# Inverse roots on GpSimd, rows copied earlier, merged weights computed in four parts of the layer before

## Chip, cores, metric

One core of one Trainium2 chip. The metric is the device time of one execution of the whole program in microseconds (us), the median of several runs; lower is better.

## What is computed

x is (8, 512, 128) in float32. First a small recurrent layer, then six layers of windowed attention and a gated feed-forward block. Cut to what matters:

```python
h = tanh(h @ A.T + xb_t); y = h @ C.T                # 512 steps in sequence, with layer norms around
for i in range(6):
    t = shift_tokens(x)                              # features 64..127 from one token earlier
    q, k, v = split(t @ Wqkv[i])                     # 16 heads of 64
    q, k = l2norm(q), l2norm(k)                      # one inverse root for each token and head
    q, k = rotary(q), rotary(k)
    attn = softmax(8 * q k^T, masked to a window of 32 and the one before)
    x = (attn @ v) @ Wo[i] + x
    t = shift_tokens(x)
    n = (t - mean) / sqrt(var + 1e-5)                # one inverse root for each token
    a, g = split(n @ W1[i] + b1[i]); x = (a * gelu(g)) @ W2[i] + b2[i] + x
```

## The kernel before

Everything is held in SBUF, the engines' programs are written out by hand, and semaphores are the only order between them. Engines are called PE (TensorE), DVE (VectorE), ACT (ScalarE), POOL (GpSimd) and SP (the queue that issues DMAs).

**Recurrence.** The first 356 us are 512 steps of a small matmul on PE (L532) and a tanh on ACT (L750), in eight chunks of 64 tokens. Two filler matmuls (`keep_warm`, L517) stand in each step, or one filler and one piece of a neighbouring chunk's work (`outputs`, `turn_input`, `turn_xn`, `start_chunk`). DVE does the layer norms of the chunks beside it.

**Layers.** The work is cut into 192 tiles of 128 tokens (a window of 32 tokens of four sequences), 32 tiles a layer. A loop over steps s runs them as a pipeline: in step s tile A = s is projected and rotated, B = s-1 is normalised, turned and compared, C = s-2 goes through the softmax, E = s-3 gets its output. Four tiles make a round T, 48 in all, and after a round its feed-forward block is run in the steps that `turn_of(s, lag)` names: lag 7 the rows and their statistics, 8 the normalised rows, 9 the turn back, 10 the gate, 11 and 12 the values, 13 the second product. So four kinds of step alternate, told apart here by s mod 4: **kind 3** (rows, statistics, value part 0), **kind 0** (normalised rows, value parts 1 and 2), **kind 1** (turn back, second product), **kind 2** (gates).

Order on each engine within a step, as far as it matters:
- PE: project q of A (L552); transpose of C (L646); output of E with merged weights (L654); turn q of B (L559); project k of A (L552); turn k of B (L559); feed-forward pieces; comparisons of B (L701); softmax times inputs of C (L714).
- ACT: copies of `px` (L822), inputs, `ex` (L828), square of q (L769), copies of turned q and k (L855, L862), values (L808), square of k, feed-forward pieces (among them `xr`, L776, the rows' copy out of PSUM, kind 3), last `guess_roots` (L812, L814), the first guess of the inverse roots of tile A.
- DVE: rotate q (L954, L957), softmax sums, sum of squares of q (L963), output added (L1024), rotate k, `pT` (L1033), statistics of rows (L985, L989, kind 3, read from PSUM), update of x (L995, kind 1), sum of squares of k, maximum, `px`, `sh` (L1054), last `inverse_roots` (L970 to L978), five operations on 32 (kind 3: 36) elements in a partition that refine the guess to `rr`.
- POOL: in kind 0 `shift` (L442); B's q and k times `rr` (L448, twice); `pn` of C (L453); sum of the two rotated halves of A's q and k (L458, twice); the tables' scales (L431, kinds 1 and 3); in kind 3 variance and mean of the rows (L467, L469); `hh`, value times gate (L477: one in kind 3, two in kind 0).

**Merged weights.** `w_vo` = Wv Wo of a head is computed on PE once a layer (L664, 16 products, 32 instructions) into four PSUM banks that the turns use too, in the single step s = 32 L + 2 (`layer_of`), and copied out by ACT (L850, four copies). PE waits for the output before (`y_added`) ahead of it and for the copies behind it. `w_vo` has one buffer.

## Time and profile before

| | us |
|---|---|
| median of 3 runs (3452.42 to 3457.12) | 3455.07 |
| profiled execution, its own time | 3451.7 |
| its span, first to last instruction | 3449.9 |
| recurrence (first L552 at 358.1) | 358 |
| 192 steps of the layers, to the last L552 | 2995 |
| end of the pipeline | 97 |

Busy shares of the span: PE 96%, PE's weight loads 62%, DVE 81%, ACT 67%, POOL 65%; mean granted TensorE clock 0.989. How to read it: the page's first part gives busy time by engine; a matmul's end is modelled and its tail overlaps the next, so busy time of PE does not by itself say that PE is the bound. What says more is the order in time of a few steps, where an engine's start stands right behind what released it. Times of the trace count from the start of the span.

### The profile page before, as it was taken

Reading aid. Unit: us, or ns where it says so; the run is one execution under the profiler, and the core shown is the slowest. Engines: PE = TensorE matmul, PEld = TensorE weight load, DVE = VectorE, ACT = ScalarE, POOL = GpSimd, SP = SyncE. Lnnn points to the kernel's source line nnn. Section 1 sums busy time; section 2 is a strip of 40 time slices with the busy share of each in tenths; the row PEclk is TensorE's granted clock in tenths of the full one; section 3 lists DMA queues with packets and bytes.
Section 4 is the critical chain, followed back from the end, with each engine's and each line's share of the span. In section 5 each row is a group of like instructions: output and inputs, shape, how many; then the busy total and the mean of one; then the engine's idle time right before and its main releaser. Section 6 shows DMA issues by size and latency. Waiting matters only on the chain. (4 is left out here: it accounts for less than half of the span.)

```text
span 3449.9 us, 100942 instructions
## 1 busy us (share of the span) xinstructions
PE 3313.6 (96%) x42197; PEld 2155.7 (62%) x42197; DVE 2796.1 (81%) x4511; ACT 2308.7 (67%) x4545; POOL 2259.3 (65%) x1364
## 2 busy tenths in 40 slices
PE   8999689999999999999999999999999999999996
PEld 5555366666666666666666666666666666666663
DVE  2333698988898899898889889988888898988892
ACT  2222367777777777777777777777777777777774
POOL 0000476777777777777777677776777776777772
PEclk9999899999999999999999999999999999999998
DMA  2000000100001000001000001000001000000000
GB/s 72 1 1 1 7 11 9 36 11 11 8 17 35 11 8 11 11 17 33 11 11 11 8 17 35 11 9 10 11 17 32 11 11 11 12 13 17 14 8 13
DMA packets 62281, 52.50 MB, mean 15 GB/s; under 512 B 11526, under 2 KB 59396, under 8 KB 61828
## 3 DMA queue, kind: packets, MB, share of 16 engines
q1 hardware_dynamic: 61828, 46.05, 5.1%
q8 instruction: 335, 5.49, 0.7%
q14 instruction: 118, 0.97, 0.1%
HBM read 43.93 MB, written 2.10 MB: 13 GB/s over the span
## 5 line engine op out<-in xcount | busy, mean ns | idle before, releaser
L448 POOL TENSOR_TENSOR cosp<-cosp,rr 128x1024 f32<-128x1024 f32 x384 | 723.2, 1905 | 587.0 <-DVE rr L978 586.9
L458 POOL TENSOR_TENSOR cosp<-cosp,sinp 128x1024 f32<-128x1024 f32 x384 | 903.4, 2375 | 53.9 <-DVE sinp L957 53.7
L552 PE MATMUL ps<-w_qk,xs 128*128 128x512 f32 x1536 | 762.5, 619 | 21.0 <-ACT sq L769 17.2
L654 PEld LDWEIGHTS ps<-px,w_vo 128*128 128x128 f32 x6144 | 701.0, 192 | 57.5 <-ACT px L822 44.2
L654 PE MATMUL ps<-px,w_vo 128*128 128x128 f32 x6144 | 721.6, 276 | 2.0 <-ACT px L822 1.7
L769 ACT ACTIVATE sq<-ps 128x1024 f32<-128x1024 f32 x384 | 393.0, 1023 | 473.5 <-DVE sinp L957 473.5
L954 DVE TENSOR_TENSOR cosp<-ps,tab 128x1024 f32<-128x1024 f32 x384 | 469.2, 1222 | 143.0 <-PE ps L552 141.6
L552 PEld LDWEIGHTS ps<-w_qk,xs 128*128 128x128 f32 x1536 | 262.9, 191 | 385.9 <-issue 376.0
L963 DVE TENSOR_REDUCE ss<-sq 128x16 f32<-128x1024 f32 x384 | 455.2, 1185 | 55.0 <-ACT sq L769 54.9
L957 DVE TENSOR_TENSOR sinp<-ps,tab 128x1024 f32<-128x1024 f32 x384 | 465.9, 1213 | 0.0
L714 PE MATMUL ps<-pT,xtm 32*128 32x512 f32 x3072 | 447.6, 625 | 12.7 <-issue 5.5
L559 PEld LDWEIGHTS ps<-ident,cosp 128*128 128x128 f32 x3072 | 354.1, 141 | 117.1 <-DVE xb L1024 73.5
L559 PE MATMUL ps<-ident,cosp 128*128 128x128 f32 x3072 | 399.4, 273 | 14.1 <-ACT w_vo L850 7.4
L453 POOL TENSOR_TENSOR pn<-ex,rsum 128x1024 f32<-128x1024 f32 x192 | 365.8, 1905 | 6.8 <-DVE rsum L1019 6.5
L701 PEld LDWEIGHTS ps<-kT,qT 64*32 64x32 f32 x24576 | 254.9, 105 | 169.9 <-issue 169.1
L822 ACT COPY px<-ps 128x512 f32<-128x512 f32 x576 | 297.9, 588 | 65.5 <-PE ps L714 65.3
L701 PE MATMUL ps<-kT,qT 64*32 64x64 f32 x24576 | 288.0, 225 | 26.4 <-issue 19.6
L517 PE MATMUL ps<-ident_bf 128*128 128x512 bf16 x912 | 280.2, 378 | 0.0
L714 PEld LDWEIGHTS ps<-pT,xtm 32*128 32x128 f32 x3072 | 174.9, 185 | 141.7 <-issue 86.8
L750 ACT ACTIVATE cosp<-ps 128x8 f32<-128x8 f32 x512 | 91.0, 178 | 244.6 <-PE ps L532 244.6
L532 PEld LDWEIGHTS ps<-cosp,qT 128*128 128x128 f32 x1024 | 155.8, 189 | 147.5 <-ACT cosp L750 140.3
L862 ACT COPY kT<-ps 128x512 f32<-128x512 f32 x384 | 206.3, 592 | 53.5 <-PE ps L559 53.5
(106 smaller groups left out, 4502.4 us busy)
## 6 DMA issues: line engine op xcount, KB each, us to landing
tab<-in_tab SPq DMA_DIRECT2D x96, 128.0 KB, 2.1
qks<-in_scales SPq DMA_DIRECT2D x96, 128.0 KB, 3.4
w_qk<-in_L_ffn_Wqkv SPq DMA_DIRECT2D x12, 512.0 KB, 6.0
w_v<-in_wv_t SPq DMA_DIRECT2D x6, 512.0 KB, 7.4
w_o<-in_L_ffn_Wo SPq DMA_DIRECT2D x6, 512.0 KB, 8.5
x<-in_L_attn_x SPq DMA_DIRECT2D x16, 128.0 KB, 4.7
out<-w_v SPq DMA_DIRECT2D x16, 128.0 KB, 2.5
w<-in_L_ffn_W SPq DMA_DIRECT2D x6, 341.0 KB
```

The costliest lines, as they stand in the source:

```text
L448: eng.tensor_tensor(v, v, rr[:, B % 2, HEADS * i:HEADS * i + HEADS].unsqueeze(2).to_broadcast([P, HEADS, DH]), ALU.mult).then_inc(rot_read ...
L453: eng.tensor_tensor(pn[:, :].rearrange("p (h k) -> p h k", k=DH), ex[:, :].rearrange("p (h k) -> p h k", k=DH), rsum[:, :].unsqueeze(2).to ...
L458: eng.tensor_tensor(cosp[:, A % 2, i, :], cosp[:, A % 2, i, :], sinp[:, i, :], ALU.add).then_inc(rot_added, 1)
L552: t = eng.matmul(ps[:, u, :], xs[:, n % ROUND, :], w_qk[:, n // TILES % 2, i, 512 * u:512 * u + 512], start=True, stop=True)
L559: t = eng.transpose(G(k)[:, 128 * m:128 * m + 128], cosp[:, n % 2, i, at:at + 128], ident[:, :])
L654: t = eng.matmul(Y, w_vo[:, i // HP, i % HP, :], px[:, i, :], start=i == 0, stop=i == HEADS - 1)
L701: t = eng.matmul(ps[32 * b:32 * b + 32, 2 + h2, DH * hp:DH * hp + DH], qT[rows, hp, 32 * b:32 * b + 32], kT[rows, B % NG, hp, b, :], start ...
L714: t = eng.matmul(G(b), xtm[rows, C % NG, k, :], pT[rows, :].rearrange("p (h k q) -> p h k q", k=2, q=WIN)[:, :, k, :], start=k == 0, stop= ...
L769: eng.activation(sq[:, i, :], R.rearrange("p a n -> p (a n)"), ACT.Square).then_inc(sq_done, 1)
L954: eng.tensor_tensor(cosp[:, n % 2, i, :].rearrange("p (h d) -> p h d", d=DH), src, cos, ALU.mult).then_inc(roped, 1)
L957: eng.tensor_tensor(sinp[:, i, :].rearrange("p (h u f) -> p h u f", u=2, f=32), swapped, sin, ALU.mult).then_inc(roped, 1)
L963: eng.tensor_reduce(ss[:, HEADS * i:HEADS * i + HEADS], sq[:, i, :].rearrange("p (h d) -> p h d", d=DH), AX_X, ALU.add).then_inc(ssq_done, 1)
```

## The change

- `inverse_roots` goes from DVE (five fused operations) to POOL (nine simple ones, since POOL has no fused form here: five `tensor_tensor`, four `tensor_scalar`). It stands last in POOL's step, behind `hh`. Every operation from the third on waits for the one before by a semaphore. POOL is also the engine that multiplies by `rr` next.
- On POOL the tables' scales (L431) are moved behind variance and mean of the rows.
- The rows' copy `xr` is issued on ACT behind the copies of turned k and waits for the rows' transposes alone; the statistics on DVE read `xr` in SBUF and wait for that copy.
- The merged weights of layer L + 1 are computed in four parts of four products (eight PE instructions) in steps of kind 0, s mod 32 = 16, 20, 24, 28, of layer L, ahead of the output's matmuls, each with one ACT copy; `w_vo` has two buffers. Those of layer 0 are computed within the recurrence, each part in place of a filler, and copied by DVE.
- The loads of the next layer's weights are issued one round earlier; `xe` takes the place of `w_o`, which is free by then.

```diff
-REFINE = 5
+REFINE = 9
...
-        w_vo = sb("w_vo", [P, 2, HP, D])
+        w_vo = sb("w_vo", [P, 2, 2, HP, D])
...
-        xe = sb("xe", [P, CH])
+        xe = w_o.rearrange("p k d -> p (k d)")[:, 0:CH]
...
-        def layer_of(s):
-            L = (s - 2) // TILES
-            return L if (s - 2) % TILES == 0 and 0 <= L < DEPTH else None
+        def fuse_of(s):
+            L, part = s // TILES + 1, s % TILES // ROUND - 4
+            return (L, part) if s % ROUND == 0 and part >= 0 and L < DEPTH else None
...
-                if L + 1 < DEPTH and T % NC == 3:
+                if L + 1 < DEPTH and T % NC == 2:
                     load_qk(L + 1)
                     load_vo(L + 1)
...
+            def inverse_roots(s, lo, hi):
+                base = normed(s)
+                x, h, guess = ss[:, lo:hi], rhalf[:, lo:hi], rguess[:, lo:hi]
+                eng.wait_ge(root_step, rooted(s) + 2)
+                eng.tensor_tensor(h, guess, guess, ALU.mult).then_inc(norm_step, 1)
+                eng.tensor_scalar(x, x, TINY, -1.0, ALU.max, ALU.mult).then_inc(norm_step, 1)
+                eng.wait_ge(norm_step, base + 2)
+                eng.tensor_tensor(x, x, h, ALU.mult).then_inc(norm_step, 1)
+                eng.wait_ge(norm_step, base + 3)
+                eng.tensor_scalar(h, x, CUBIC[0], None, ALU.add).then_inc(norm_step, 1)
+                eng.wait_ge(norm_step, base + 4)
+                eng.tensor_tensor(h, h, x, ALU.mult).then_inc(norm_step, 1)
+                eng.wait_ge(norm_step, base + 5)
+                eng.tensor_scalar(h, h, CUBIC[1], None, ALU.add).then_inc(norm_step, 1)
+                eng.wait_ge(norm_step, base + 6)
+                eng.tensor_tensor(h, h, x, ALU.mult).then_inc(norm_step, 1)
+                eng.wait_ge(norm_step, base + 7)
+                eng.tensor_scalar(h, h, CUBIC[2], None, ALU.add).then_inc(norm_step, 1)
+                eng.wait_ge(norm_step, base + 8)
+                eng.tensor_tensor(rr[:, s % 2, lo:hi], h, guess, ALU.mult).then_inc(norm_step, 1)
...
-                    if A % ROUND == 1:
-                        scale_table(1, A // ROUND)
-                    if A % ROUND == 3 and A + 1 < NT:
-                        scale_table(0, A // ROUND + 1)
                 T = turn_of(s, 7)
                 if T is not None:
                     eng.wait_ge(stat_step, 2 * TB * T + 2 * TB)
...
                     eng.tensor_scalar(ss[:, 2 * HEADS:], aggr[:, :, 1], EPS, SPREAD, ALU.add, ALU.mult).then_inc(variance_done, 1)
                     after(eng, shift_done, T)
                     eng.tensor_scalar(nmean[:, :], aggr[:, :, 0], -1.0, None, ALU.mult).then_inc(variance_done, 1)
+                if tile(A):
+                    if A % ROUND == 1:
+                        scale_table(1, A // ROUND)
+                    if A % ROUND == 3 and A + 1 < NT:
+                        scale_table(0, A // ROUND + 1)
...
+                T = turn_of(s, 7)
+                if tile(A):
+                    inverse_roots(s, 0, 2 * HEADS + (TB if T is not None else 0))
+                elif T is not None:
+                    inverse_roots(s, 2 * HEADS, 2 * HEADS + TB)
...
+            def fuse(L, part):
+                if part == 0:
+                    eng.wait_ge(wv_in, 16 * (L + 1))
+                    eng.wait_ge(wo_in, 16 * (L + 1))
+                if L == 0:
+                    after(eng, vo_evac, part)
+                for i in range(2 * part, 2 * part + 2):
+                    for x in range(2):
+                        rows = slice(64 * x, 64 * x + 64)
+                        t = eng.matmul(ps[:, 5 + x if L else 2 + 4 * x, D * (i % 2):D * (i % 2) + D], w_v[rows, i, :], w_o[rows, i, :], start=True, stop=True)
+                t.then_inc(vo_done, 1)
...
+                    elif t == AT_FUSE and c - 3 in range(4):
+                        fuse(0, c - 3)
...
+                    if fuse_of(s):
+                        fuse(*fuse_of(s))
                     if E % TILES == 0:
                         eng.wait_ge(vo_evac, 4 * (E // TILES + 1))
                     after(eng, y_added, E)
                     for i in range(HEADS):
-                        t = eng.matmul(Y, w_vo[:, i // HP, i % HP, :], px[:, i, :], start=i == 0, stop=i == HEADS - 1)
+                        t = eng.matmul(Y, w_vo[:, E // TILES % 2, i // HP, i % HP, :], px[:, i, :], start=i == 0, stop=i == HEADS - 1)
                     t.then_inc(y_done, 1)
-                L = layer_of(s)
-                if L is not None:
-                    eng.wait_ge(wv_in, 16 * (L + 1))
-                    eng.wait_ge(wo_in, 16 * (L + 1))
-                    after(eng, y_added, E + 1)
-                    eng.wait_ge(xt_evac, C + 1)
-                    for i in range(HP):
-                        for x in range(2):
-                            t = eng.matmul(G(2 * x + i // 4)[:, D * (i % 4):D * (i % 4) + D], w_v[64 * x:64 * x + 64, i, :],
-                                           w_o[64 * x:64 * x + 64, i, :], start=True, stop=True)
-                            if i % 4 == 3:
-                                t.then_inc(vo_done, 1)
                 if tile(B):
-                    if L is not None:
-                        eng.wait_ge(vo_evac, 4 * (L + 1))
+                    if fuse_of(s):
+                        L, part = fuse_of(s)
+                        eng.wait_ge(vo_evac, 4 * L + part + 1)
...
-                T = turn_of(s, 7)
-                if T is not None:
-                    eng.wait_ge(stat_step, 2 * TB * T + TB)
-                    after(eng, xn_ready, TB * T)
-                    eng.copy(xr[:, :, :].rearrange("p j d -> p (j d)"), G(1)).then_inc(rows_evac, 1)
...
+                if fuse_of(s):
+                    L, part = fuse_of(s)
+                    eng.wait_ge(vo_done, 4 * L + part + 1)
+                    after(eng, y_done, TILES * (L - 1))
+                    eng.copy(w_vo[:, L % 2, :, 2 * part:2 * part + 2, :], ps[:, 5:7, 0:2 * D].rearrange("p x (i d) -> p x i d", d=D)).then_inc(vo_evac, 1)
...
-                L = layer_of(s)
-                if L is not None:
-                    for k in (0, 2, 1, 3):
-                        eng.wait_ge(vo_done, 4 * L + (2 if k % 2 == 0 else 4))
-                        eng.copy(w_vo[:, k // 2, 4 * (k % 2):4 * (k % 2) + 4, :].rearrange("p i d -> p (i d)"), G(k)).then_inc(vo_evac, 1)
...
+                T = turn_of(s, 7)
+                if T is not None:
+                    eng.wait_ge(rows_done, T + 1)
+                    after(eng, xn_ready, TB * T)
+                    eng.copy(xr[:, :, :].rearrange("p j d -> p (j d)"), G(1)).then_inc(rows_evac, 1)
...
+                if c - 3 in range(4):
+                    part = c - 3
+                    eng.wait_ge(vo_done, part + 1)
+                    for x in range(2):
+                        t = eng.tensor_copy(w_vo[:, 0, x, 2 * part:2 * part + 2, :].rearrange("p i d -> p (i d)"), ps[:, 2 + 4 * x, 0:2 * D])
+                    t.then_inc(vo_evac, 1)
...
-            def inverse_roots(s, lo, hi):
-                base = normed(s)
-                x, h, guess = ss[:, lo:hi], rhalf[:, lo:hi], rguess[:, lo:hi]
-                eng.wait_ge(root_step, rooted(s) + 2)
-                eng.scalar_tensor_tensor(out=h, in0=guess, scalar=-1.0, in1=guess, op0=ALU.mult, op1=ALU.mult).then_inc(norm_step, 1)
-                eng.wait_ge(norm_step, base + 1)
-                eng.scalar_tensor_tensor(out=x, in0=x, scalar=TINY, in1=h, op0=ALU.max, op1=ALU.mult).then_inc(norm_step, 1)
-                eng.wait_ge(norm_step, base + 2)
-                eng.scalar_tensor_tensor(out=h, in0=x, scalar=CUBIC[0], in1=x, op0=ALU.add, op1=ALU.mult).then_inc(norm_step, 1)
-                eng.wait_ge(norm_step, base + 3)
-                eng.scalar_tensor_tensor(out=h, in0=h, scalar=CUBIC[1], in1=x, op0=ALU.add, op1=ALU.mult).then_inc(norm_step, 1)
-                eng.wait_ge(norm_step, base + 4)
-                eng.scalar_tensor_tensor(out=rr[:, s % 2, lo:hi], in0=h, scalar=CUBIC[2], in1=guess, op0=ALU.add, op1=ALU.mult).then_inc(norm_step, 1)
-
             def statistics(T):
                 base = 2 * TB * T
-                eng.wait_ge(rows_done, T + 1)
+                eng.wait_ge(rows_evac, T + 1)
                 after(eng, stat_step, base)
                 for i in range(TB):
-                    eng.bn_stats(stat[:, i, :], G(1)[:, P * i:P * i + P]).then_inc(stat_step, 1)
+                    eng.bn_stats(stat[:, i, :], xr[:, i, :]).then_inc(stat_step, 1)
...
-                if tile(A):
-                    after(eng, rot_ready, 2 * (A - 1))
-                    inverse_roots(s, 0, 2 * HEADS + (TB if T7 is not None else 0))
-                elif T7 is not None:
-                    inverse_roots(s, 2 * HEADS, 2 * HEADS + TB)
```

## Rows read from the trace of the kernel before

**Rows 1.** The page, part 1: busy time and share of the span by engine.
```profile
PE 3313.6 (96%) x42197; PEld 2155.7 (62%) x42197; DVE 2796.1 (81%) x4511; ACT 2308.7 (67%) x4545; POOL 2259.3 (65%) x1364
```
**Rows 2.** Waits: engine and line, releaser: us in total, times, longest us.
```profile
POOL cosp L448 <- DVE rr L978: 586.9, 145, 9.3
...
PEld ps L714 <- ACT xr L776: 30.5, 36, 0.9
```
**Rows 3.** Windows: stretch, length, busy of five engines, clock, DMA share, GB/s.
```profile
1503.08:1519.18 16.10, 15.83 (x215) 10.41 (x211) 14.81 (x20) 9.98 (x19) 12.65 (x8) 1.00 0.15 34
1519.18:1534.72 15.54, 15.54 (x212) 10.39 (x208) 13.47 (x18) 13.20 (x23) 10.29 (x5) 1.00 0.06 18
1534.72:1550.06 15.34, 15.27 (x211) 9.94 (x208) 14.39 (x26) 11.55 (x22) 12.10 (x9) 1.00 0.06 19
1550.06:1564.33 14.27, 14.27 (x207) 9.53 (x205) 12.69 (x18) 10.73 (x21) 11.72 (x8) 1.00 0.01 3
...
553.41:3306.80 2753.39, 2696.09 (x36698) 1784.64 (x36696) 2439.57 (x3568) 2016.71 (x3632) 2058.59 (x1233) 1.00 0.06 16
```
**Rows 4.** Timeline of PE, kinds 2 and 1: start, length, engine, line, [idle before].
```profile
1524.69 1.04 PE L559 MATMUL ps<-ident,cosp 128*128 128x128 f32 x8
1525.70 1.53 PE L552 MATMUL ps<-w_qk,xs 128*128 128x512 f32 x3
...
1570.02 1.04 PE L559 MATMUL ps<-ident,cosp 128*128 128x128 f32 x8
1571.32 1.95 PE L552 MATMUL ps<-w_qk,xs 128*128 128x512 f32 x4 [0.27 <-ACT sq L769]
1573.11 1.04 PE L559 MATMUL ps<-ident,cosp 128*128 128x128 f32 x8
1573.99 0.60 PE L579 MATMUL ps<-ident,xn 128*128 128x128 f32 x4
```
**Rows 5.** Windows: the step in which layer 1's merged weights are computed.
```profile
892.86:914.30 21.44, 17.25 (x243) 11.80 (x239) 13.59 (x18) 15.60 (x27) 10.35 (x5) 1.00 0.01 2
```
**Rows 6.** Timeline of PE in that step.
```profile
901.46 2.06 PE L664 MATMUL ps<-w_o,w_v 64*128 64x128 f32 x32 [2.93 <-DVE xb L1024]
```
**Rows 7.** Timeline of POOL, kinds 3, 0 and the start of 1.
```profile
1537.80 3.77 POOL L448 TENSOR_TENSOR cosp<-cosp,rr 128x1024 f32<-128x1024 f32 x2 [5.21 <-DVE rr L978]
...
1548.04 0.73 POOL L431 TENSOR_TENSOR tab<-tab,qks 128x256 f32<-128x256 f32 x1
1548.85 0.19 POOL L467 TENSOR_SCALAR ss<-aggr 128x4 f32<-128x4 f32 x1
1549.12 0.22 POOL L469 TENSOR_SCALAR nmean<-aggr 128x4 f32<-128x4 f32 x1
1549.31 1.26 POOL L477 TENSOR_TENSOR hh<-aa,ge 128x512 f32<-128x512 f32 x1
1553.12 0.20 POOL L442 TENSOR_TENSOR shift<-nmean,rr 128x4 f32<-128x4 f32 x1 [2.55 <-DVE rr L978]
1553.27 3.77 POOL L448 TENSOR_TENSOR cosp<-cosp,rr 128x1024 f32<-128x1024 f32 x2
...
1563.51 2.50 POOL L477 TENSOR_TENSOR hh<-aa,ge 128x512 f32<-128x512 f32 x2
1567.93 3.77 POOL L448 TENSOR_TENSOR cosp<-cosp,rr 128x1024 f32<-128x1024 f32 x2 [1.93 <-DVE rr L978]
```
**Rows 8.** Timeline of DVE: the last refining operation of a tile.
```profile
1567.66 0.19 DVE L978 SCALAR_TENSOR_TENSOR rr<-rhalf,rguess 128x32 f32<-128x32 f32 x1
```
**Rows 9.** Timeline of ACT: the guess that ends kind 2's step.
```profile
1534.50 0.32 ACT L814 ACTIVATE rguess<-rclamp,guess_at 128x32 f32<-128x32 f32 x1
```
**Rows 10.** Windows: a step of kind 3 with a long comparison.
```profile
722.10:738.67 16.57, 14.38 (x210) 9.73 (x207) 14.48 (x26) 11.29 (x21) 12.61 (x9) 1.00 0.08 17
```
**Rows 11.** Timeline of the end: PE resumes behind a POOL product.
```profile
3374.39 3.76 POOL L448 TENSOR_TENSOR cosp<-cosp,rr 128x1024 f32<-128x1024 f32 x2
...
3378.30 1.06 PE L559 MATMUL ps<-ident,cosp 128*128 128x128 f32 x8 [0.73 <-POOL cosp L448]
```

More of the change, by code:

```diff
@@ L116 @@
 KEEP = 512
-AT_OUTPUT, AT_INPUT, AT_XN, AT_START = 3, 38, 46, 58
+AT_OUTPUT, AT_FUSE, AT_INPUT, AT_XN, AT_START = 3, 24, 38, 46, 58
 DMA_W1 = 1 + 2 * len(FT)
@@ L546, in _ @@
                 outputs(NC - 1, j)
+            eng.wait_ge(vo_evac, 4)
             def project(n, i):
@@ L886, in read_result @@
                 eng.wait_ge(x_updated, DEPTH * NC + c + 1)
+                eng.wait_ge(vo_done, 4 * DEPTH)
                 after(eng, end_turned, c)
```

## Prediction

> **What bounds the kernel now.** I read the page's busy shares first: PE is at 96%, DVE at 81%, POOL at 65% [rows 1]. Since a busy PE can still be a waiting PE, I then read the order in time. A round of four steps takes 61.25 us, and PE is busy for 60.91 of them, POOL for 46.8 [rows 3]. In PE's timeline each piece starts where the one before lets it, with few exceptions: in kind 1 project k starts 1.30 behind turn q, where turning k leaves 0.88 to what follows (0.42 lost to the late square of q); in kind 2 the same gap is 1.01 (0.13 lost) [rows 4]; in kind 3 the last stage waits 0.85 for the rows' copy [rows 2]. So PE bounds the steps, and its waits that can be removed are about 1.4 of 61.25 us. Once a layer there is a large one: the step with the merged weights takes 21.44 where its kind takes 15.54, 5.9 more [rows 3, 5], with PE idle for 2.93 ahead of the 2.06 of L664 and waiting again for the copies behind it [rows 6].
>
> The longest line of the waits is POOL's for `rr`, 587 us in 145 waits [rows 2], on an engine that is not the bound. It is slack, and the change spends it. How much is there in each step is the question: 5.21 us in kind 3, 2.55 in kind 0, 1.93 in kind 1 [rows 7].
>
> **The roots on POOL, price.** No row shows a 32-element operation there. A `tensor_tensor` takes 0.20 on 4 elements (L442) and 0.73 on 256 (L431), so 0.0021 an element and 0.26 on 32 [rows 7]. A `tensor_scalar` on 4 elements takes 0.19 with two operations and 0.22 with one [rows 7]; with one input I give it half that slope, so 0.22 and 0.25. Between operations: L431 ends at 1548.77 and L467 starts at 1548.85, L467 ends at 1549.04 and L469 starts at 1549.12, and POOL starts 0.08 behind DVE's last operation (1567.85 to 1567.93) [rows 7, 8]. I take 0.08 for POOL's wait for itself. R = 5 x 0.262 + 0.22 + 3 x 0.25 + 8 x 0.08 = 2.92 us (0.262 unrounded), and 0.07 more with 36 elements. DVE's five are 0.19 long each, 0.95 in all without the gaps [rows 8].
>
> Bounds of R. From below: L448 starts only 0.15 behind the start of the 0.20 long L442, so a reported length can overstate what an operation costs; with spacings, 0.15 + 0.06 for a product and 0.27 + 0.03 for a `tensor_scalar`, R = 5 x 0.21 + 4 x 0.30 = 2.25. From above: PE starts 0.15 behind the end of a POOL product (L448 ends at 3378.15, L559 starts at 3378.30) [rows 11]; if POOL's own wait costs that, R = 3.48. I take 2.92, because every gap around a `tensor_scalar` and every wait of POOL in the rows is 0.08.
>
> **What the roots do to a round.** I follow POOL from the guess that ends kind 2's step [rows 9], with the old times beside the new.
> - Kind 3. Guess ready at 1534.82, roots start 0.08 later, L448 0.08 behind them: 1537.90, before 1537.80. PE needs the first product (1.90 us) 5.5 us after its step's start, at 1540.2, and gets it at 1539.95. Nothing is lost. From L448 to the end of `hh` POOL has no gap but 0.08s: 12.77 us, before as after (order alone changes) [rows 7]. End 1550.67.
> - Kind 0. The guess is ready before that, so the roots run straight on, 0.05 into the end as L448 does behind L442: 1550.62 + 2.99, then `shift` (0.08 + 0.15), L448 at 1553.84; before 1553.27. POOL's 2.55 of slack is gone. Then 12.74 us without a gap (1553.27 to 1566.01): 1566.58.
> - Kind 1. 1566.53 + 2.92 + 0.08: L448 at 1569.53, before 1567.93. PE turns q at 1569.53 + 1.90 + 0.15 = 1571.58, before 1570.02: 1.56 later. Project k follows after 0.88 and not 1.30, so it is 1.14 late; the gap of 0.13 in kind 2 goes too, leaving 1.01.
> - Kind 2. Here POOL has slack again: kind 3's 5.21 us of idle time are the rest of a step in which the guess comes late from PE and ACT. The chain runs from PE's project k over DVE and ACT to the guess as before, and closes there, 1.0 us late.
>
> The round takes 61.25 + 1.0 = 62.25 us. It holds three times R on its path, so it moves by 3 us for each us of R: 45 rounds, 135 us per us. Below R = 2.58 the change of the round is a gain.
>
> **DVE relieved.** Rotating q starts about 0.9 earlier in each step. That removes the two PE gaps named (0.42, 0.13), which are in the sum above. Otherwise DVE waits for PE's project k anyway.
>
> **Early rows and tables.** ACT's copy of 512 elements now lies ahead of the value and the square of k; DVE reaches the statistics only behind `pT`, after the copy, so nothing is late. PE's 0.85 in kind 3 goes, and PE then reaches turn q of kind 0 at about 1554.5, where the product comes at 1555.9: the gain ends in that wait and I count it at nothing. Variance and mean move ahead of the table's scale, which ends some 0.6 us later (0.08 + 0.19 + 0.08 + 0.22) and which DVE first reads in the next step. SP's loads come a round earlier, behind waits long met: nothing.
>
> **Merged weights.** The six steps lose their 5.9: -35.4 us. The work comes back as eight instructions in a kind 0 step, a quarter of 2.06, 0.5 us, and one ACT copy where there were four in one step. They lie in the 1.4 us that PE waits for the product in kind 0, so they cost nothing; without that wait they would cost 24 x 0.5 = 10 to 12 us. For layer 0 four slots of the recurrence get 0.5 longer: +2.
>
> **Irregular stalls.** The 44 rounds from 553 to 3307 take 2753.4, that is 58.4 over 44 x 61.25 [rows 3]; 29.5 are layer steps, 29 are single stalls of PE among the comparisons, such as a kind 3 step of 16.57 instead of 15.34 [rows 10]. 22 such steps over 0.3 us are of kinds 3 and 0 and hold 24 us of it. After the change PE waits 1.4 in kind 0 and 1.5 in kind 1 for POOL, behind just these stretches, so a stall of up to 1.4 is swallowed: -23.
>
> **Ends.** The first two rounds have no `hh` and a PE step of 14 us, and roots on POOL are in their loop: +2. At the end the last rows' four roots are alone on the path, 1.5 longer: +1.5.
>
> **Sum.** Against the profiled execution: 3451.7 + 45 x 1.0 - 35.4 - 23 + 2 + 2 + 1.5 = 3443.8. The median of the runs lies 3.4 above that execution, so I put the time at 3447.
>
> **A rule against.** By the rows the roots cost about three times on POOL what they cost on DVE. The Trainium skill (GPSIMD Engine Reference, section Engine selection) says to keep elementwise work on VectorE, GpSimd being about twice as slow with two inputs; twice 0.95 would be 1.9, the round would come down to PE's own (61.25 less 0.42, 0.13 and 0.85, 59.85) and the total to 3447 - 45 x 2.4 = 3339. The same notes (Perfetto Trace Analysis, GPSIMD Engine Instruction) say that reported GpSimd lengths are unreliable and spacing is to be used; the 0.15 between L442 and L448 agrees for independent operations, and no row shows it for a dependent one. Both speak for the second rival.
>
> **Rivals.**
> - Slower: POOL's wait for its own semaphore costs more than a wait for DVE. At 0.15, R = 3.48 and the round gets 0.56 x 3 more: +76 us, 3523. Beyond R = 3.03, 0.014 more for each of eight waits, the kernel is slower by more than 0.2%. For it: nine short operations in a chain are what no row shows. Against: all gaps of 0.08.
> - Faster: an operation costs its spacing, R = 2.25. The round is then 60.24, total 3447 - 90 = 3357; at R = 2.6 it is 3404. For it: L442 and L448. Against: a dependent operation has to see the end of the one before.
> - The spread weights are not free: the copy waits on ACT behind `ex`, or PE has no wait in kind 0 to hide them. Then some 12 to 20 of the 35 us come back: 3460 to 3467. Against: the guess, not ACT's copy, is late in kind 0.
> - The change does not do what it says: stalls swallowed by nothing (+23): 3470. It is part of the forecast's own range.
>
> **How the numbers follow.** Forecast, R from 2.75 to 3.1, 3424 to 3471: chance 0.5. Slower rival, 3471 to 3523: 0.24. Faster rival, 3357 to 3424: 0.14; PE's own bound, R under 2.2, 3339: 0.04. Weights not free: 0.08. A measurement of this kernel tells about 0.2%, 7 us. Of the forecast's half, 0.25 is faster than 3448, 0.15 within, 0.10 slower; with the rivals faster 0.43, same 0.21, slower 0.36. The range that leaves about 0.08 out on each side is 3395 to 3500.
>
> **What would show it.** In the profile after: the nine operations of one tile from first start to last end (2.9; 36-wide 3.0); no idle time of POOL from the guess of kind 2 to L448 of kind 1; PE's turn of q in kinds 0 and 1 waiting over 1 us for L448; a round of 62.25; the step s = 32 L + 2 as long as others of kind 2; no wait of L714 for `xr`. A round of 59.5 to 60.5 would say that R is small and PE the bound; one above 63 that POOL's self-wait is dear. Wrong, too, would be a granted clock that falls because PE now pauses: before, the step with 2.93 of PE idle kept 1.00 [rows 5, 6].

## Result and profile after

| | before | after |
|---|---|---|
| median of 6 runs each, same chip | 3456.38 (3452.42 to 3465.97) | 3436.23 (3434.89 to 3438.67) |
| ratio, 95% interval | | 0.9938 [0.9925, 0.9951] |
| profiled execution, its span | 3451.7, 3449.9 | 3435.68, 3433.9 |
| busy PE, DVE, ACT, POOL | 96, 81, 67, 65% | 94, 77, 67, 80% |

The kernel is 0.6% faster, 20 us; 3447 was forecast, 8 us under the median that the forecast started from. The page's first part, as [rows 1] of before; POOL has 1737 instructions more:

```profile
PE 3241.3 (94%) x42193; PEld 2123.9 (62%) x42193; DVE 2636.4 (77%) x3554; ACT 2316.9 (67%) x4541; POOL 2736.0 (80%) x3101
```

The windows of one round, kinds 3, 0, 1 and 2, and of the same 44 rounds as the last line of [rows 3] (columns as there). The round has a part of the merged weights in it. The line that starts at 890.03 is the step with s = 32 L + 2 that took 21.44 us in [rows 5]:

```profile
1718.03:1731.82 13.79, 13.77 (x211) 9.63 (x208) 12.30 (x20) 10.54 (x18) 12.91 (x15) 1.00 0.10 21
1731.82:1748.19 16.37, 15.41 (x217) 10.05 (x214) 12.98 (x15) 12.23 (x24) 15.53 (x20) 1.00 0.01 2
1748.19:1765.35 17.16, 15.83 (x216) 10.42 (x212) 13.95 (x15) 10.06 (x19) 15.87 (x19) 1.00 0.06 17
1765.35:1780.33 14.98, 14.98 (x212) 9.88 (x208) 12.72 (x13) 13.41 (x23) 12.38 (x13) 1.00 0.01 3
...
890.03:905.02 14.99, 14.99 (x212) 9.89 (x208) 12.72 (x13) 13.41 (x23) 12.38 (x13) 1.00 0.01 2
...
1718.03:1780.33 62.30, 59.99 (x843) 39.99 (x839) 51.96 (x61) 46.24 (x83) 56.69 (x64) 1.00 0.04 11
545.04:3294.54 2749.50, 2632.46 (x36701) 1754.94 (x36697) 2292.68 (x2690) 2027.32 (x3634) 2495.25 (x2820) 1.00 0.06 16
```

Kinds 3 and 2 are now PE's own length (13.79 of 13.79 busy, 14.98 of 14.98), kinds 0 and 1 hold PE's waits: 0.96 and 1.33 us. POOL is busy for 15.87 of 17.16 us of kind 1. The round is 1.05 longer than before (62.30 against 61.25), yet the 44 rounds are 3.9 us shorter: what a typical round lost, the layer steps and the irregular time gave back.

POOL's timeline of the same round, from kind 3's end to kind 2's start (start, length, engine, line, operation; idle time before it in brackets, where there is any). It answers [rows 7], where POOL idled for 2.55 and 1.93 us:

```profile
1732.81 1.27 POOL L499 TENSOR_TENSOR hh<-aa,ge 128x512 f32<-128x512 f32 x1
1734.04 0.24 POOL L439 TENSOR_TENSOR rhalf<-rguess 128x36 f32<-128x36 f32 x1
...
1737.34 0.20 POOL L463 TENSOR_TENSOR shift<-nmean,rr 128x4 f32<-128x4 f32 x1
1737.50 3.77 POOL L469 TENSOR_TENSOR cosp<-cosp,rr 128x1024 f32<-128x1024 f32 x2
1741.22 1.91 POOL L474 TENSOR_TENSOR pn<-ex,rsum 128x1024 f32<-128x1024 f32 x1
1743.08 4.70 POOL L479 TENSOR_TENSOR cosp<-cosp,sinp 128x1024 f32<-128x1024 f32 x2
1747.74 2.50 POOL L499 TENSOR_TENSOR hh<-aa,ge 128x512 f32<-128x512 f32 x2
1750.20 0.23 POOL L439 TENSOR_TENSOR rhalf<-rguess 128x32 f32<-128x32 f32 x1
...
1753.08 0.25 POOL L454 TENSOR_TENSOR rr<-rhalf,rguess 128x32 f32<-128x32 f32 x1
1753.42 3.77 POOL L469 TENSOR_TENSOR cosp<-cosp,rr 128x1024 f32<-128x1024 f32 x2
...
1764.84 0.24 POOL L439 TENSOR_TENSOR rhalf<-rguess 128x32 f32<-128x32 f32 x1 [0.45 <-ACT rguess L842]
```

Each operation starts where the one before lets it; the first idle time is 0.45 us at 1764.84. And PE's timeline of kinds 0 and 1 beside it:

```profile
1734.24 0.72 PE L543 MATMUL ps<-w_o,w_v 64*128 64x128 f32 x8
1734.88 3.84 PE L698 MATMUL ps<-px,w_vo 128*128 128x128 f32 x32
1739.55 1.06 PE L601 MATMUL ps<-ident,cosp 128*128 128x128 f32 x8 [0.82 <-POOL cosp L469]
...
1755.38 1.09 PE L601 MATMUL ps<-ident,cosp 128*128 128x128 f32 x8 [1.33 <-POOL cosp L469]
```

The first of POOL's two products (1.90 us) ends at 1755.32 and PE turns q at 1755.38. The waits of the whole execution say it in sums (us, times, longest); the line of L448 for `rr` that headed [rows 2] is gone, and so is that of L714 for `xr`:

```profile
POOL rhalf L439 <- ACT rguess L842: 118.1, 94, 8.2
PE ps L601 <- POOL cosp L469: 101.3, 90, 6.2
```

### The profile page after: what moved, and what is told of

Its sections match the earlier page's. It is cut to its first block and busy times, and to the rows that moved or that the text cites. A ratio compares the mean times of both kernels' runs of the same rounds, so it can differ in the third digit from the quotient of the medians.

```text
span 3433.9 us, 101546 instructions
## 1 busy us (share of the span) xinstructions
PE 3241.3 (94%) x42193; PEld 2123.9 (62%) x42193; DVE 2636.4 (77%) x3554; ACT 2316.9 (67%) x4541; POOL 2736.0 (80%) x3101
## 5 line engine op out<-in xcount | busy, mean ns | idle before, releaser
L594 PE MATMUL ps<-w_qk,xs 128*128 128x512 f32 x1536 | 748.1, 610 | 9.8 <-ACT sq L802 6.1
L601 PE MATMUL ps<-ident,cosp 128*128 128x128 f32 x3072 | 404.8, 275 | 101.3 <-POOL cosp L469 101.3
L747 PE MATMUL ps<-pT,xtm 32*128 32x512 f32 x3072 | 393.3, 614 | 12.4 <-DVE w_v L1029 5.5
L427 POOL COPY px<-cosp 128x512 f32<-128x512 f32 x8 | 8.8, 1104 | 345.5 <-ACT cosp L783 345.5
L883 ACT COPY qT<-ps 128x512 f32<-128x512 f32 x384 | 207.2, 593 | 82.2 <-PE ps L601 80.2
```

The source lines that it names most:

```text
L594: t = eng.matmul(ps[:, u, :], xs[:, n % ROUND, :], w_qk[:, n // TILES % 2, i, 512 * u:512 * u + 512], start=True, stop=True)
L601: t = eng.transpose(G(k)[:, 128 * m:128 * m + 128], cosp[:, n % 2, i, at:at + 128], ident[:, :])
L747: t = eng.matmul(G(b), xtm[rows, C % NG, k, :], pT[rows, :].rearrange("p (h k q) -> p h k q", k=2, q=WIN)[:, :, k, :], start=k == 0, stop= ...
```

## Experiments

Each was timed against the kernel before on the same chip, and the ratio is to that. "Round" is the typical one, the sum of the median lengths of the four kinds. In the kernels with the spread weights kind 0 is longer when it holds a part of them; after, e5 and e6 are given with a part, e2 without. The choice moves a row by at most 0.7 us (e7 is 62.30 with a part and 61.67 without).

| | median | ratio, 95% | round | 44 rounds |
|---|---|---|---|---|
| before | | | 61.25 | 2753.4 |
| after | 3436.23 | 0.9938 [0.9925, 0.9951] | 62.29 | 2749.5 |
| e1 roots on POOL alone | 3462.91 | 1.0026 [1.0013, 1.0039] | 62.24 | 2769.7 |
| e2 weights alone | 3430.06 | 0.9942 [0.9924, 0.9961] | 61.25 | 2741.1 |
| e3 early rows alone | 3441.65 | 0.9973 [0.9963, 0.9983] | 60.92 | 2754.8 |
| e4 all but the roots | 3402.80 | 0.9865 [0.984, 0.989] | 60.95 | 2714.8 |
| e5 two operations more | 3552.77 | 1.0275 [1.0259, 1.029] | 64.53 | 2856.3 |
| e6 two operations fewer | 3357.33 | 0.9712 [0.9697, 0.9726] | 60.41 | 2674.7 |
| e7 e4, roots ahead of `px` | 3434.07 | 0.9933 [0.9918, 0.9948] | 61.81 | 2749.9 |
| e8 after, `hh` a step later | 3389.98 | 0.9802 [0.9783, 0.9821] | 61.0 | 2702.4 |
| e9 e4, roots early in two kinds | 3392.08 | 0.9801 [0.9775, 0.9826] | 60.50 | 2706.0 |

The question of the first four runs: what is each part worth, and do the parts need each other?

**e1: the roots on POOL and nothing else.** The kernel before with the new `inverse_roots` in place of the old one:

```diff
-                if tile(A):
-                    after(eng, rot_ready, 2 * (A - 1))
-                    inverse_roots(s, 0, 2 * HEADS + (TB if T7 is not None else 0))
...
+                T = turn_of(s, 7)
+                if tile(A):
+                    inverse_roots(s, 0, 2 * HEADS + (TB if T is not None else 0))
```

> The kernel before with nothing but the inverse roots moved to GpSimd (nine operations, last in its step); merged weights and rows stay as they were. Theory (GpSimd becomes the chain from kind 2's guess to kind 1's product): the round is the 62.3 us of the changed kernel, because the rows' copy does not lie on that chain, and the layer steps keep their 5.9 us: 3436 + 34 = about 3468 us, slower than before by 0.3%. The nine operations last 3.14 us. Rival (the relief of VectorE is itself a gain, the slack of GpSimd covers the roots): at or below 3456 minus 48 x 0.5, 3430 us or less.

Measured 3462.91, 0.26% more than before. The roots on POOL are a loss by themselves. PE in the step with layer 1's merged weights:

```profile
902.19 2.06 PE L690 MATMUL ps<-w_o,w_v 64*128 64x128 f32 x32 [1.71 <-DVE xb L1036]
905.50 1.09 PE L585 MATMUL ps<-ident,cosp 128*128 128x128 f32 x8 [1.26 <-ACT w_vo L876]
```

The wait for DVE's output has fallen from 2.93 to 1.71 [rows 6], because DVE is relieved, but the step stays 5.2 us longer than its kind. Only the spreading removes it.

**e2: the merged weights spread and nothing else.**

```diff
+                    if fuse_of(s):
+                        fuse(*fuse_of(s))
...
-                L = layer_of(s)
-                if L is not None:
-                    eng.wait_ge(wv_in, 16 * (L + 1))
```

> The kernel before with the merged weights alone changed (four parts in kind 0 steps, two buffers, layer 0 in the recurrence; the tables' scale behind variance and mean goes with it, the roots stay on VectorE). Theory: -35 us for the six steps, +2 in the recurrence, and since PE has no wait in kind 0 to hide eight instructions, +0.5 us in each of 20 steps: about 3433 us. Rival (the parts are hidden even with PE as the bound): 3423. Rival (the ACT copy delays the square of q and so project k): 3445 or more.

Measured 3430.06, with 3433 expected: the weights alone give what the whole change gives (0.9942 and 0.9938). Here PE has no wait in kind 0 to hide a part in: a round without a part takes 61.25, one with a part 61.94, so 20 parts give back some 14 us.

**e3: the early rows and nothing else.**

```diff
 (ACT, behind the copies of turned k)
+                T = turn_of(s, 7)
+                if T is not None:
+                    eng.wait_ge(rows_done, T + 1)
+                    after(eng, xn_ready, TB * T)
+                    eng.copy(xr[:, :, :].rearrange("p j d -> p (j d)"), G(1)).then_inc(rows_evac, 1)
...
-                    eng.bn_stats(stat[:, i, :], G(1)[:, P * i:P * i + P]).then_inc(stat_step, 1)
+                    eng.bn_stats(stat[:, i, :], xr[:, i, :]).then_inc(stat_step, 1)
```

> The kernel before with the early copy of the rows alone (copy behind the turned k, statistics from SBUF; roots on VectorE, weights as before). Theory (PE is the bound, the wait of the last stage in kind 3 is 0.85 to 1.1 us of each of 48 rounds): 3456 - 41 to 54 = 3402 to 3415 us. Rival (square of k and guess come later by the copy's 0.6 us and the gain is given back in kind 0): 3440 to 3456.

Measured 3441.65: my theory missed, the rival held. Kind 3 loses its wait for `xr` (15.34 to 14.20), but kind 0 takes back most of it (14.27 to 15.08). The windows of kinds 3 and 0:

```profile
1538.89:1553.09 14.20, 14.16 (x211) 9.67 (x208) 13.33 (x26) 10.50 (x19) 11.04 (x7) 1.00 0.07 20
1553.09:1568.17 15.08, 14.80 (x210) 9.54 (x206) 13.63 (x19) 11.69 (x23) 12.81 (x10) 1.00 0.02 4
```

ACT and PE at the start of kind 0:

```profile
1553.26 0.32 ACT L807 ACTIVATE rclamp<-ss,guess_at 128x36 f32<-128x36 int32 x1 [1.59 <-POOL ss L467]
1553.62 0.33 ACT L809 ACTIVATE rguess<-rclamp,guess_at 128x36 f32<-128x36 f32 x1
1553.85 1.54 ACT L817 COPY px<-ps 128x512 f32<-128x512 f32 x3
...
1555.44 3.84 PE L654 MATMUL ps<-px,w_vo 128*128 128x128 f32 x32
```

The same two in the kernel before, where kind 0 starts at 1550.06 [rows 3]:

```profile
1549.08 0.32 ACT L812 ACTIVATE rclamp<-ss,guess_at 128x36 f32<-128x36 int32 x1 [0.99 <-POOL ss L467]
...
1551.98 3.74 PE L654 MATMUL ps<-px,w_vo 128*128 128x128 f32 x32
```

The guess stands ahead of `px` on ACT and waits for the rows' variance from POOL. Before, it began 0.98 ahead of the step's start, now 0.17 behind it: PE's step ends 1.1 us sooner and the chain to the guess does not. So the output starts 2.35 after the step's start instead of 1.92, and turn q and project k are later still. What PE saves in kind 3 it waits for in kind 0. The 44 rounds of this execution are no shorter than before (2754.8 against 2753.4) although the typical round is; it spent 30.7 us of them at half clock, the one before 13.7 (see the clock, below).

**e4: everything but the roots on POOL.** The kernel after with `inverse_roots` of before.

```diff
+                if tile(A):
+                    after(eng, rot_ready, 2 * (A - 1))
+                    inverse_roots(s, 0, 2 * HEADS + (TB if T7 is not None else 0))
...
-                T = turn_of(s, 7)
-                if tile(A):
-                    inverse_roots(s, 0, 2 * HEADS + (TB if T is not None else 0))
```

> The changed kernel with the inverse roots put back on VectorE (five fused operations, last in its step), all else as changed. Theory (the roots on GpSimd are what holds the round at 62.3, and they eat the other two gains): PE is the bound, a round of about 60.2 us, and the sum of the other two parts alone, 3380 us (3370 to 3390), faster than both kernels. Rival (the parts need each other: with the roots on VectorE the early rows and the spread weights gain little): 3430 or more.

Measured 3402.80, by the ratios 0.7% less than after. It missed its forecast of 3380 mostly for e3's reason: a round of 60.95 where 60.2 was expected. Weights and rows together save 1.35%, apart 0.58 and 0.27%: in e4 a part of the weights stands in the time in which `px` is late in kind 0 and costs under 0.1 us (15.11 with a part, 15.05 without) where in e2 it cost 0.7. So two of the three parts help each other, and the third takes 0.7% back.

The next two runs ask whether R, the chain of nine, is what bounds the round, as the forecast had it.

**e5 and e6: two dependent operations more, two fewer.**

```diff
 (e5, behind the last tensor_scalar)
+                eng.tensor_scalar(h, h, 1.0, None, ALU.mult).then_inc(norm_step, 1)
+                eng.wait_ge(norm_step, base + 9)
+                eng.tensor_scalar(h, h, 1.0, None, ALU.mult).then_inc(norm_step, 1)
+                eng.wait_ge(norm_step, base + 10)
...
 (e6)
-                eng.tensor_tensor(h, h, x, ALU.mult).then_inc(norm_step, 1)
-                eng.wait_ge(norm_step, base + 7)
-                eng.tensor_scalar(h, h, CUBIC[2], None, ALU.add).then_inc(norm_step, 1)
-                eng.wait_ge(norm_step, base + 8)
```

> The changed kernel with two operations more in the chain of the roots (two products of a value with 1.0, each waiting for the one before, 0.37 us each: 0.29 long and 0.08 behind). Theory (the chain from kind 2's guess to kind 1's product holds three times R): R from 3.14 to 3.88, the round from 62.3 to 64.5, the time + 45 x 2.2 = 3436 + 100 = 3536 us. Rival (the roots hold up only one step of four, once R): + 33 us, 3470. Rival (PE bounds the changed kernel): within 10 us of 3436.

> The changed kernel with two operations fewer in the chain of the roots (the last coefficient of the cubic and one product are left out, so the inverse roots and with them the output are not exact). Theory: R 2.46 instead of 3.14 (0.26 and 0.29 long, 0.08 behind each), the round 62.3 - 2.0 = 60.3, the time 3436 - 90 = 3346 us. Where another bound comes first, the time stops above that: the merged weights lose their cover and cost up to 10 us, single stalls are no longer swallowed and give back up to 20 us, so 3346 to 3376. Rival (once R per round): 3405.

Measured 3552.77 and 3357.33, with 3536 and 3346 to 3376 expected. (e6 leaves out a coefficient of the cubic, so its output is not exact; it serves the timing alone.) The 17 us of e5 above its expectation are what its profiled execution lost in ten steps with the clock at half. The same round as above in both, e5 first:

```profile
1769.49:1834.01 64.52, 60.20 (x842) 40.02 (x838) 51.96 (x61) 46.30 (x84) 58.93 (x72) 1.00 0.04 10
```
```profile
1683.62:1744.02 60.40, 59.80 (x842) 39.96 (x839) 51.95 (x61) 46.24 (x83) 54.54 (x56) 1.00 0.04 11
```

PE is busy for 60.20 and 59.80 us of them, so only its waits move. R is 3.89 (4.00 with 36 elements), 3.14 (3.23) in after and 2.43 (2.50) in e6; three of them, one with 36, make 11.78, 9.51 and 7.36. The round goes 64.53, 62.29, 60.41: 0.99 us for each us of that sum upward, 0.87 downward. The forecast's "three times R" holds, and below R = 3.14 the gain starts to flatten towards PE's own 59.8 to 60.

Two runs then look for a better place for the roots, on either engine.

**e7: e4 with the roots ahead of `px` on DVE.**

```diff
+                if tile(A):
+                    after(eng, rot_ready, 2 * (A - 1))
+                    inverse_roots(s, 0, 2 * HEADS + (TB if T7 is not None else 0))
...
                 if tile(C):
                     eng.wait_ge(px_done, 4 * C + 4)
                     after(eng, y_done, C)
```

> The run with the roots back on VectorE, with these five operations moved in VectorE's order from behind `sh` to ahead of its copy of `px`, into idle time of 0.9 us. Theory: rotating q starts about 0.9 us earlier, PE loses the gaps ahead of project k (0.35, 0.43, 0.14, 0.1 in kinds 0, 1, 2, 3) and the lateness of ACT in kind 2 (0.35): 60.9 - 1.2 = 59.7 us a round, 3403 - 55 = 3348 us. Rival (in kind 1, where the guess comes 0.5 us after PE's step starts, `px` is late by that and the output's matmuls with it): 0.4 to 0.8 of it lost again, 3370 to 3390; `px` late in every step: 3403 or more.

Measured 3434.07, by the ratios 0.7% more than e4, against a forecast of 3348. DVE and PE at the start of kind 1:

```profile
1499.41 0.82 DVE L984 SCALAR_TENSOR_TENSOR rhalf<-rguess 128x32 f32<-128x32 f32 x1
...
1501.06 0.68 DVE L1069 COPY px<-ps 128x512 f32<-128x512 f32 x1
...
1501.84 0.35 PE L672 MATMUL ps<-px,w_vo 128*128 128x128 f32 x1 [1.04 <-issue]
```

DVE's share of `px` is a copy that the output waits for, and it now stands behind the roots: 1.65 us from the first of them to `px`. PE idles for 1.04 ahead of the output, and kinds 0 and 1 take 15.80 and 16.70 against 15.07 and 16.11. The first operation alone took 0.82 where its kind takes 0.18; the last section has that. In kind 2 the step did get shorter (15.08 against 15.54): the idea is right where `px` is not the last thing that the output waits for.

**e8: after, with `hh` on POOL moved a step later, behind the products.** The roots stay on POOL.

```diff
-                    T = turn_of(s, lag)
+                    T = turn_of(s, lag + 1)
...
 (the loop over VALUES now stands here)
+                        eng.tensor_tensor(hh[0:fn, m, :], aa[0:fn, m, :], ge[0:fn, m, :], ALU.mult).then_inc(glu_done, 1)
                 if tile(C):
                     eng.wait_ge(recip_done, C + 1)
                     after(eng, p_turned, C)
```

> The changed kernel (roots on GpSimd) with `hh` moved in GpSimd's order from the end of a step to the next step behind the two products with the roots. Theory: the three `hh` products (3.7 us) leave the chain from kind 2's guess to kind 1's product, which becomes shorter than PE's work; in kinds 3 and 0 the roots then wait for the guess instead; the round falls from 62.3 to 59.5 to 60.5 and the time to 3436 - 80 to 125, 3311 to 3356 us, plus 10 to 20 for stalls no longer swallowed. Rival (GpSimd's whole load of 59.5 us a round, or `pn` late by the 2.5 us of the two `hh`, is the next bound): the round stays above 61.5, 3400 us or more.

Measured 3389.98, by the ratios 1.4% below after. It lies between my theory (3376 at most, a round of 59.5 to 60.5) and the rival (3400 or more, a round above 61.5); the round is 61.0. The waits of the whole execution:

```profile
POOL rhalf L439 <- ACT rguess L842: 81.8, 70, 8.2
...
PE ps L601 <- POOL cosp L469: 34.4, 69, 6.2
```

PE's wait for POOL's product has fallen from 101.3 to 34.4 us. It did not go altogether: `hh` now stands in kind 1, where the table's scale also stands, and POOL is full there instead.

```profile
1742.82 0.74 POOL L431 TENSOR_TENSOR tab<-tab,qks 128x256 f32<-128x256 f32 x1
1743.51 0.25 POOL L439 TENSOR_TENSOR rhalf<-rguess 128x32 f32<-128x32 f32 x1
...
1748.69 1.09 PE L601 MATMUL ps<-ident,cosp 128*128 128x128 f32 x8 [0.48 <-POOL cosp L469]
```

The guess of this tile was there at 1741.98 (L842), the roots start at 1743.51, and PE waits 0.48 in kind 2 (POOL's and PE's timeline above). By kind, PE's waits for POOL's product in the 44 rounds are 2.8, 1.2 and 18.2 us in kinds 0, 1 and 2, where after has 37.6, 51.0 and none. Besides, `hh` itself is now late for PE's second product (36 waits, 9.9 us in all). Kinds 0 and 1 take 15.10 and 16.21 against 16.24 and 17.15 in after, kind 2 takes 15.69 against 14.98. Moving 2.5 us of work moved the saturated stretch, it didn't end it. I had counted no wait in kind 2; that was the miss.

**e9: e4 with the roots early in kinds 1 and 2 only**, the two boundaries at which e7 said they do no harm.

```diff
-                if tile(A):
+                if tile(A) and s % ROUND not in (1, 2):
...
+                if tile(A) and s % ROUND in (1, 2):
+                    after(eng, rot_ready, 2 * (A - 1))
+                    inverse_roots(s, 0, 2 * HEADS)
```

> The run with the roots on VectorE ahead of `px`, but so only for the guesses that end the steps of kinds 1 and 2, when GpSimd is idle; those of kinds 3 and 0 stay behind `sh`. Theory (in the run with all four early, the first of the five operations was held for 0.6 us by the `hh` product on GpSimd, and `px` and the output's matmuls behind it came 1.3 us late in kinds 0 and 1): kinds 0 and 1 as with the late roots (15.07, 16.1), kinds 2 and 3 as with the early ones (15.1, 14.2), a round of 60.5 us, 3403 - 20 = 3383 us. The first operation is 0.18 us long in every step. Rival (the lateness comes from the place alone, whatever GpSimd does): steps of kinds 2 and 3 lose as well, 3403 or more.

Measured 3392.08, the kinds at 15.11, 16.11, 15.07 and 14.23 as expected. The median is 9 above the 3383 forecast. That no run settles, but the profiled execution (3397.95, the slowest of the four) spent 27.3 us of its 44 rounds at half clock where e4's spent 3.4, which costs up to 12 us. e8 and e9 can't be told apart (0.9802 and 0.9801) and both beat the kernel after by 1.4%, e8 with the roots on POOL, e9 with them on DVE. In this kernel the engine that refines the roots matters less (0.7%, after against e4) than what stands before them in its queue (1.4%, e8 against after).

## Why the prediction was right, point by point

3447 was forecast, 3436 measured, and the time was 0.3% below the forecast. The gain is another matter: 8 us were forecast and 20 measured. And part of the agreement is luck. The measured R, 3.14, lies outside the 2.75 to 3.1 on which the forecast's range stood; put into the prediction's own sum it gives 3447 + 135 x 0.22 = 3477, a kernel slower than before, in the range of the slower rival. That the kernel is faster all the same comes mostly from terms that the prediction did not have: 0.65 us a round that DVE's relief and a shorter hand-over gave back, a slow end in the execution before, and less time at half clock. By the steps of the prediction:

**What bounds.** Right: PE's chain, with POOL's idle time as slack that the change spends. POOL is without a gap from the guess of kind 2 to the product of kind 1, and PE waits for it in kinds 0 and 1 alone. The forecast put those waits at 1.4 and 1.5; they are 1.4 without a part of the weights (0.82 with one) and 1.33.

**The price R.** Mis-sized: 3.14 us, not 2.92. By line, POOL's nine operations (busy us in all, mean ns; the 36-wide ones are in the mean):

```profile
L440 POOL TENSOR_SCALAR ss<-ss 128x32 f32<-128x32 f32 (+1 forms) x193 | 64.2, 333 | 16.3
...
L452 POOL TENSOR_SCALAR rhalf<-rhalf 128x32 f32<-128x32 f32 (+1 forms) x193 | 56.3, 292 | 16.9
L454 POOL TENSOR_TENSOR rr<-rhalf,rguess 128x32 f32<-128x32 f32 (+1 forms) x193 | 49.4, 256 | 16.1
```

The idle time over the count is 0.083 to 0.088 us: POOL's wait for itself costs the 0.08 that every gap before had shown, so the slower rival's mechanism (0.15) did not show. Nor does the faster one's: a dependent operation costs its whole length, not its spacing. The five `tensor_tensor` came to 1.26 (1.31 forecast). The error is the four `tensor_scalar`, 1.22 against 0.97: I had rows of 4 elements alone and gave them half the slope of two inputs, which no run bears out. Three times 0.22 is +0.66 us on the round, 30 us on the kernel. That POOL has no fused form, as the description of the change has it, no run here tests; the kernel does put two operations with constants (`max`, `mult`) into one `tensor_scalar`, L440.

Of the Trainium skill's rule that was weighed against this (GPSIMD Engine Reference, Engine selection: about twice as slow with two inputs): the chain takes 3.14 us on POOL and 1.09 on DVE, 2.9 times, since nine operations stand for five and each waits. Operation by operation it is less than the page's two: 0.25 us for two inputs on POOL against 0.19 on DVE. And of its caution about reported GpSimd lengths (Perfetto Trace Analysis, GPSIMD Engine Instruction): lengths plus 0.08 a wait add up to the measured R here.

**The round.** Forecast 62.25, measured 62.29, and right by two errors that cancel. Against the +0.66 of R stand two things that I had not counted. POOL's product is followed by PE within 0.06 us (1755.32 to 1755.38, and so in 71 of 90 waits), not within the 0.15 of [rows 11], which the other waits show. And kind 2's guess comes 0.56 earlier behind project k. ACT in kind 2 of after:

```profile
1769.82 1.02 ACT L802 ACTIVATE sq<-ps 128x1024 f32<-128x1024 f32 x1 [1.18 <-DVE sinp L997]
...
1771.83 1.08 ACT L883 COPY qT<-ps 128x512 f32<-128x512 f32 x2
1772.93 1.28 ACT L886 ACT_TABLE_LOAD   x1
...
1779.96 0.32 ACT L842 ACTIVATE rguess<-rclamp,guess_at 128x32 f32<-128x32 f32 x1
```

Project k starts at 1771.72 and the guess ends at 1780.28, 8.56 later; before, 1525.70 [rows 4] and 1534.82 [rows 9], 9.12. The prediction said "The chain runs from PE's project k over DVE and ACT to the guess as before". It doesn't: DVE, relieved of 1.1 us of roots, finishes the halves of q 0.7 earlier, so ACT's whole row of work behind the square of q, a table load of 1.28 in it, is 0.7 earlier, and it was late enough to hold PE's gates and the last stage. I had read the relief of DVE only in the two PE gaps it leaves behind q, not in ACT. The runs bear out that it is the roots' leaving DVE that shortens kind 2: it takes 14.98 in e1, where nothing else changed, and 15.54 in e4, where they are on DVE.

**Early rows at nothing.** Right in after: kind 3 is at PE's own 13.79 and the wait behind it takes the gain. e1, with the roots on POOL and the rows late as before, has the same round (62.24): kind 3 takes 15.17 there and kind 0 14.90. e3 shows that it would have been worth only 0.33 a round in any case, not the 0.85 of the wait that it removes.

**Merged weights, -35.4.** Right. The step at 890.03 takes 14.99 and is an ordinary one of its kind. The part in kind 0 is hidden: PE's wait for the product is 0.82 with it and 1.4 without. e2 puts a price on that cover, 14 us, where the prediction had 10 to 12. Layer 0's step was worth no more than the others: the first 12 steps take 184.8 against 195.3, but steps 1, 2 and 4, in which its weights show, give 4.3 of the 10.5 us (5.7 in e2). Another 3.4 lie in steps 9 and 10, where the execution before has PE idle for 2.39 us and then 6.8 us at half clock (517.5 to 524.3), and after, e2 and e4 have no such stretch.

**Stalls swallowed, -23.** Right in the main: 44 times 62.29 is 2740.8, so all irregular time in them is 8.7 us, where before it was 28.9 beside the layer steps, 20 less. Up to 6.8 us of that is not a stall swallowed but time at half clock that the execution before had and after had not (the clock, below); three of the 22 steps from which the 23 was taken have such a stretch in them. The stalls are still there, 24 of kinds 3 and 0 with 28 us, but their next step is shorter. Two windows, a kind 3 with a stall of 1.51 among the comparisons, and the kind 0 behind it:

```profile
1592.80:1608.23 15.43, 13.92 (x211) 9.69 (x207) 13.58 (x21) 11.19 (x20) 14.47 (x18) 1.00 0.07 19
1608.23:1623.20 14.97, 14.97 (x218) 10.04 (x214) 11.89 (x13) 11.59 (x22) 14.21 (x17) 1.00 0.01 3
```

Together 30.40 us where the undisturbed pair above takes 30.16 (13.79 and 16.37): of 1.6 us, 0.25 is left. The same sum is 5 to 18 us in the runs in which PE waits for POOL's product (e1, e5, e6, e8), and 29 to 44 in those in which it does not (before, e2, e3, e4, e7, e9; layer steps and parts of the weights taken off). That tells the mechanism, and that it belongs to the waits for POOL. The clock doesn't make this difference: e4 has 33 us of irregular time with 3.4 us at half clock, e5 has 17 with 34.1 us, which account for all of it. Where the stalls themselves come from I did not test.

**Ends.** The start is 2.1 later (360.28 against 358.15; +2 forecast). The end is 4.5 shorter, where I had +1.5. At least part of that is the clock of the execution that I had profiled before: its last 53.9 us have a granted clock of 0.77, those of after 0.84, and its last full step already fell to half. From the start of that step on it spends 27.7 us at half clock and after 17.0, which is worth up to 5.3 us. That stage in PE's timeline of before, and its window:

```profile
3367.47 3.69 PE L714 MATMUL ps<-pT,xtm 32*128 32x512 f32 x16
```
```profile
3367.47:3370.80 3.33, 3.33 (x23) 1.16 (x16) 1.29 (x2) 0.65 (x2) 0.53 (x1) 0.52 0.40 79
```

A clock of 0.52 is 1.2 GHz for nearly all of it; the same 16 instructions take 2.00 at 2.4 GHz. In the nine experiments the end took 91.3 to 95.1, wherever the roots stood, against 97.1 in that execution and 92.6 after: the forecast took an end at a low clock for the usual one. The last rows' roots cost nothing visible: from the end of the turn of the last rows to their turn back 9.3 us pass, 9.7 before, where the clock was lower. Their copy goes earlier by about what the roots add, I argue; no run separates the two.

The sum against the profiled executions: +2.1 before the first step, -10.5 in the first 12, -3.9 in the 44 rounds, +0.8 in the steps to the last and -4.5 at the end, -16.0 in all, for a forecast of -7.9. The 8 us between them are the first 12 steps (7 of them) and the end (6), against 5 in the 44 rounds.

**The clock.** In after it did not fall once the first three steps were over: 1.00 from 410 to 3396 us, with PE idle for 0.82 and 1.33 us in kinds 0 and 1. Before, it did, and neither the description nor the prediction saw it. In the 44 rounds it was at half, 1.2 GHz, in four stretches, 13.7 us in all; three of them follow waits of PE of 2.94, 2.52 and 2.05 us. The prediction took from one layer step that 2.93 us of idle PE leave the clock at 1.00. The layer step of layer 3's weights has the same wait, and its 32 instructions took 3.47 us instead of 2.06:

```profile
1900.31 3.47 PE L664 MATMUL ps<-w_o,w_v 64*128 64x128 f32 x32 [2.94 <-DVE xb L1024]
```
```profile
1899.90:1903.30 3.40, 2.99 (x28) 3.02 (x30) 0.15 (x1) 0.87 (x2) 3.17 (x2) 0.50 0.00 0
```

Time at half clock in the 44 rounds, in us: before 13.7, after, e1 and e6 none, e2 10.2, e3 30.7, e4 3.4, e5 34.1, e7 17.1, e8 3.4, e9 27.3. From the first step to the end it is 78.9 before and 44.3 in after. If PE was the bound in all of it, the difference is worth 17 us, which is an upper estimate and as large as the 16 us between the two executions. The mean granted clock of after's six executions is 0.991 to 0.994, that of the executions before, e3 and e5 mostly 0.985 to 0.990. Whether the change keeps the clock up or the executions fell out so is not shown; e5, which waits for POOL more than after does, has the most.

## What to carry to other kernels

Idle time on an engine is a price list, not a gift: follow the chain once around a whole round before you spend it, because a chain of dependent short operations moved to the slower engine counts as often as it stands in the stretch without a gap (three times here). Take the parts of a change apart: here the weights and the rows gave 1.35%, the roots took 0.7% of it back, and moving one neighbour in the queue, 2.5 us of `hh`, gave twice what the whole change gave. A wait on one engine absorbs irregular stalls elsewhere, so a longer typical round can still make the total shorter; compare many rounds, not one. And look for the stretches at half clock before calling irregular time a stall, in the profile before above all.

## What the runs showed of the hardware

**A DVE operation held by GpSimd.** In e7 the same operation, two inputs in SBUF and 32 elements, took 0.82 and 0.18 us. While POOL computes `hh`:

```profile
1497.68 2.51 POOL L478 TENSOR_TENSOR hh<-aa,ge 128x512 f32<-128x512 f32 x2
```

L984 starts at 1499.41 and ends at 1500.23; POOL's `hh` ends at 1500.19. With POOL idle, a step later:

```profile
1515.22 0.18 DVE L984 SCALAR_TENSOR_TENSOR rhalf<-rguess 128x32 f32<-128x32 f32 x1
```

By line and shape, L984 has a mean of 367 ns over 145 of 32 elements and 600 over 47 of 36, L988, a later one of the chain, 192. In e4, where the roots come when POOL is waiting for them, L984 has 180, and in e9, which puts them early only when POOL is idle, 186; kinds 0 and 1 are then back at 15.11 and 16.11. The Trainium skill (SBUF — State Buffer, Who interferes with whom) says that DVE's second port is shared with GpSimd as an exclusive lock, so that the instruction that comes second is held; the end of L984 right behind the end of `hh` agrees.

**Short operations on GpSimd.** On 32 elements in a partition a `tensor_tensor` takes 0.242 to 0.256 us and a `tensor_scalar`, with one input, 0.292 to 0.333: the one with fewer inputs is the dearer. A wait for its own last result adds 0.08.
